# Inverse roots of the layer norms computed by Newton steps on the vector engine

## The reference, cut to what matters

```python
xn = _layernorm(x, axis=-1)
x = x + _L0_gnn_ref(xn, edge_index, ...) + _L0_mix_ref(xn[None], ...)[0]
# in _L0_gnn_ref: three times gat_conv (gather by src, softmax by dst, sum by dst), elu, layer_norm
# in _L0_mix_ref:
q = (x @ Wq + bq).reshape(...)            # k and v the same way from xn
kv = jnp.einsum('blhd,blhe->bhde', _phi(k), v)
out = attention of _phi(q) with kv, @ Wo + bo
x = _layernorm(x + out, ln1_g, ln1_b)
ff = jax.nn.relu(x @ W1 + b1) @ W2 + b2
x = _layernorm(x + ff, ln2_g, ln2_b)
```

## Time and profile before

| | |
|---|---|
| time, median of 3 runs | 7684.07 us (7683.78 to 7686.03) |
| the profiled execution: time, span | 7691.76 us, 7690.0 us |
| busy share PE, PEld, DVE, ACT, POOL | 70%, 52%, 65%, 56%, 51% |
| layer 0 message stage | about 450 to 1650 us of the span |
| layer 1 message stage | about 1950 to 3150 us |
| layer 2 message stage | about 3400 to 4600 us |

### The profile page before, as it was taken

The page is one execution under the profiler, slowest core; times in us unless marked ns, Lnnn a source line. Parts: engine busy times, 40 slices in busy tenths (PEclk is TensorE's granted clock), DMA queues, the critical chain, the costliest instruction groups (busy, mean ns, idle before and its releaser), DMA issues. The chain is left out here.

```text
span 7690.0 us, 106452 instructions
## 1 busy us (share of the span) xinstructions
PE 5415.3 (70%) x24694; PEld 4030.1 (52%) x24694; DVE 5030.4 (65%) x13781; ACT 4268.1 (56%) x13681; POOL 3924.3 (51%) x3916
## 2 busy tenths in 40 slices
PE   1757777744677777437777750899997888887678
PEld 1634444423455555325555530899994466665335
DVE  5555555666567676756666657777773387778673
ACT  4457777864688888548778773455554422111132
POOL 3276666646767677467666753000000277777322
PEclk7867788876789898768888885999998898887789
DMA  6243333333444444343433333100005644333302
GB/s 169 76 126 103 103 101 104 103 82 122 137 112 113 112 113 111 87 145 108 111 106 108 110 79 109 48 19 20 20 20 184 221 121 123 108 106 99 94 21 74
DMA packets 492760, 774.99 MB, mean 101 GB/s; under 512 B 86759, under 2 KB 368311, under 8 KB 492279
## 3 DMA queue, kind: packets, MB, share of 16 engines
q0 software_dynamic: 168240, 452.12, 21.5%
q1 hardware_dynamic: 324183, 319.65, 13.2%
HBM read 634.42 MB, written 146.27 MB: 102 GB/s over the span
## 5 line engine op out<-in xcount | busy, mean ns | idle before, releaser
L1679 POOL DMA_INDIRECT gm_got<-scratch_feat,keep_src_tab x2520 | 2503.7, 994 | 1091.7 <-issue 633.0
L1885 ACT ACTIVATE gm_got<-gm_got 128x64 f32<-128x64 f32 x10080 | 2453.1, 335 | 4.7 <-DVE gm_got L1813 4.7
L1933 PE MATMUL gm_bank<-gm_got,gm_onehot 128*128 128x264 f32 x5040 | 1844.7, 479 | 773.7 <-DVE gm_onehot L1836 429.2
L1933 PEld LDWEIGHTS gm_bank<-gm_got,gm_onehot 128*128 128x128 f32 x5040 | 1028.4, 228 | 1250.8 <-issue 647.9
L1830 DVE TENSOR_TENSOR gat_acc<-gat_acc,gm_bank 128x264 f32 x2520 | 1074.6, 426 | 706.3 <-PE gm_bank L1933 436.9
L1014 POOL DMA_INDIRECT mix1a_got<-scratch_rel_feat,layer_rel_tab x240 | 244.7, 1020 | 1397.7 <-issue 1396.7
L1014 POOL DMA_INDIRECT mix1b_got<-scratch_rel_feat,layer_rel_tab x600 | 608.6, 1014 | 190.8 <-issue 187.5
L1064 PE MATMUL mix1b_m_bank<-mix1b_got,mix1b_onehot 128*128 128x256 f32 x1200 | 398.0, 468 | 159.3 <-DVE layer_acc L1041 122.0
L1836 DVE TENSOR_TENSOR gm_onehot<-keep_iota_row,keep_dst_tab 128x896 f32<-128x896 f32 x360 | 385.7, 1080 | 27.7 <-PE gm_bank L1933 24.9
L1064 PEld LDWEIGHTS mix1b_m_bank<-mix1b_got,mix1b_onehot 128*128 128x128 f32 x1200 | 252.0, 228 | 269.6 <-DVE mix1b_onehot L1021 171.3
L3017 ACT ACTIVATE moe_h<-moe_first,moe_shift,moe_gain 128x256 f32<-128x256 f32 x400 | 203.7, 559 | 253.7 <-PE moe_first L3058 253.7
(11 more groups left out here) (559 smaller groups left out, 12232.8 us busy)
## 6 DMA issues: line engine op xcount, KB each, us to landing
scratch_rel_feat<-rel_out SPq DMA_DIRECT2D x50, 1024.0 KB, 5.5
gm_got<-scratch_feat,keep_src_tab POOLq DMA_INDIRECT x2520, 2.8
gm_flags<-scratch_flags SPq DMA_DIRECT2D x90, 280.0 KB
gf_feat<-scratch_feat SPq DMA_DIRECT2D x75, 256.0 KB, 4.1
gf_old<-scratch_hidden SPq DMA_DIRECT2D x75, 256.0 KB, 4.7
scratch_hidden<-gf_h SPq DMA_DIRECT2D x75, 256.0 KB, 3.6
scratch_feat<-gf_row SPq DMA_DIRECT2D x50, 260.0 KB, 3.5
gm_x<-scratch_x SPq DMA_DIRECT2D x50, 256.0 KB
```

Of the source, the lines that this page charges most:

```text
L1679: nc.gpsimd.indirect_dma_start(out=got[:, place // GROUPS, place % GROUPS * GROUP + j, 0:GAT_ROW], out_offset=None, in_=dram["feat"][layer ...
L1885: last = nc.scalar.activation(rows, rows, ACT.Copy, scale=got[:, b, i, D + h:D + h + 1])
L1933: nc.tensor.matmul(bank[i % BANKS][:, 0:GAT_SUM], onehot[:, i % HOTS, :], got[:, v[1] % B, i, :], start=True, stop=True).then_inc(s_sum, 1)
```

## The change

The square roots on ACT and the reciprocals on DVE go. DVE works out the inverse root itself: a first guess from the bits of the number (5 instructions: add epsilon, times -0.5, shift, conversion, subtraction), then three Newton steps of 3 instructions. Each of the 14 is counted with `Count.done`, so each waits for the one before it. They work on 128x2 values in `MixSums` and on 128x4 in `MixPairs`, where the two norms of an iteration share them.

`MixSums` puts them at slots 3, 5, 6 and 7 of each window, and copies mean and inverse root of its pair into a tile `moments` (two instructions at slot 9). `MixPairs` reads these for the first norm, so its `stats0`, `aggr0`, `root0` and first reciprocal go; the 14 instructions for the other two norms stand at slots 38, 39, 41 and 42. A tile of zeros is replaced by a part of the one-hot tile, and `mv` is set to one at the start of a stage.

```diff
+class InverseRoot:
+    PER = 14
+    PARTS = ("guess", "step1", "step2", "step3")
...
+    def part(self, nc, name, variance):
+        c, v, half, root, t, bits = self.count, self.v, self.half, self.root, self.t, self.bits
+        if name == "guess":
+            c.done(nc.vector.tensor_scalar(v[:, :], variance, LN_EPS, None, ALU.add))
+            c.done(nc.vector.tensor_scalar(half[:, :], v[:, :], -0.5, None, ALU.mult))
+            c.done(nc.vector.tensor_single_scalar(bits[:, :], v[:, :].bitcast(I32), 1, ALU.arith_shift_right))
+            c.done(nc.vector.tensor_copy(t[:, :], bits[:, :]))
+            c.done(nc.vector.tensor_scalar(root[:, :].bitcast(I32), t[:, :], -1.0, float(0x5F3759DF), ALU.mult, ALU.add))
+        else:
+            c.done(nc.vector.tensor_tensor(t[:, :], root[:, :], root[:, :], ALU.mult))
+            c.done(nc.vector.tensor_tensor(t[:, :], t[:, :], half[:, :], ALU.mult))
+            c.done(nc.vector.scalar_tensor_tensor(root[:, :], t[:, :], 1.5, root[:, :], ALU.add, ALU.mult))
...
 class MixSums:
-    DVE_AT = {0: "stats", 4: "add", 2: "aggr", 9: "scale", 19: "neg", 24: "phi"}
-    ACT_AT = {6: "root", 13: "turn", 19: "va0", 21: "exp", 23: "va1"}
+    DVE_AT = {0: "stats", 2: "aggr", 3: "guess", 4: "add", 5: "step1", 6: "step2", 7: "step3", 9: "scale", 19: "neg", 24: "phi"}
+    ACT_AT = {13: "turn", 19: "va0", 21: "exp", 23: "va1"}
...
         elif name == "scale":
-            dve.wait_ge(self.s_std, n)
-            nc.vector.reciprocal(self.rstd[:, :], self.std[:, :]).then_inc(self.s_rstd, 1)
-            dve.wait_ge(self.s_rstd, n)
...
             last.then_inc(self.s_xn, 1)
+            pair = bass.ds(it[0] * (2 * PAIR) + self.pair_no(it, t // WINDOW) * PAIR, PAIR)
+            nc.vector.tensor_copy(self.moments[:, 0, pair], self.mv[:, :, 0])
+            nc.vector.tensor_copy(self.moments[:, 1, pair], rstd[:, :])
...
-        if name == "root":
-            act.wait_ge(self.s_mv, n)
-            nc.scalar.activation(self.std[:, :], self.mv[:, :, 1], ACT.Sqrt, bias=keep["eps"][:, 0:1]).then_inc(self.s_std, 1)
...
 class MixPairs:
-    DVE_AT = {0: ["stats0"], 2: ["aggr0"], 11: ["scale0"], ...
-              ... 37: ["aggr1"], 38: ["centre1"], 40: ["centre2"],
+    DVE_AT = {9: ["scale0"], ...
+              ... 37: ["aggr1"], 38: ["centre1", "guess"], 39: ["step1"], 40: ["centre2"], 41: ["step2"], 42: ["step3"],
...
-    ACT_AT = {8: ["root0"], 15: ["turn"], 20: ["exp"], 30: ["att_turn"], 41: ["root1", "root2"], 48: ["y1_turn"],
+    ACT_AT = {15: ["turn"], 20: ["exp"], 30: ["att_turn"], 48: ["y1_turn"],
...
+            if name == "scale0":
                 dve.wait_ge(self.s_x, it[0] * 16 + (it[1] + 1) * 16)
+                for i in range(PAIR):
+                    mean, rstd = (self.moments[:, j, bass.ds(...)] for j in range(2))
+                    last = nc.vector.tensor_scalar(self.xn[:, i, :], self.x[:, i, :], mean, rstd, ALU.subtract, ALU.mult)
...
     def finish(self, dve, j, n, out, shift):
         dve.wait_ge(self.s_cen[j], n)
-        dve.wait_ge(self.s_rstd[j], n)
```

More of the change, by code:

```diff
@@ L1242, with __init__ @@
     PE_AT |= {t: [f"down{k}"] for k, t in enumerate((2, 3, 4, 5, 6, 7, 8, 9, 12, 13, 16, 17, 18, 19, 23, 24))}
-    BACK = {"add2", "stats2", "aggr2", "centre2", "finish2", "total", "root2", "relu3"} | {f"down{k}" for k in range(16)}
-    def __init__(self, nc, space, io, dram, keep, cfg, kv_sum, ones, first_pair, n_pairs):
+    BACK = {"add2", "stats2", "aggr2", "centre2", "finish2", "total", "relu3"} | {f"down{k}" for k in range(16)}
+    def __init__(self, nc, space, io, dram, keep, cfg, kv_sum, moments, ones, first_pair, n_pairs):
         sb, sem = space.sb, space.sem
@@ L1263, in __init__ @@
         self.z = sb("z", [P, PAIR * 8])
[L1264 to L1267 removed]
+        self.inverse = InverseRoot(space, 2 * PAIR)
+        self.stats = sb("stats", [P, 2, PAIR, 6])
+        self.mv = sb("mv", [P, 2, PAIR, 2])
         self.bank = [space.ps(f"side{i}", [P, 512]) for i in range(3)]
@@ L1297, in names @@
             return []
-        return [n for n in at.get(t, ()) if tags == "both" or (tags == "back") == (n in self.BACK)]
+        return [n for n in at.get(t, ()) if tags == "both" or n in InverseRoot.PARTS or (tags == "back") == (n in self.BACK)]
     def number(self, it, name):
@@ L1343, in start_dve @@
         dve.wait_ge(self.s_w, 16 * len(self.loads))
+        nc.vector.memset(self.mv[:, :, :, :], 1.0).then_inc(self.s_ones, 1)
+        dve.wait_ge(self.s_ones, 1)
         for a in range(HALVES):
@@ L1352, in dve @@
             n = self.number(it, name)
-            if name == "stats0":
+            if name == "scale0":
                 dve.wait_ge(self.s_x, it[0] * 16 + (it[1] + 1) * 16)
-                self.statistics(0, self.x)
-            elif name == "aggr0":
-                self.aggregate(dve, 0, n)
-            elif name == "scale0":
-                self.invert(dve, 0, n)
-                dve.wait_ge(self.s_rstd[0], n)
                 for i in range(PAIR):
-                    last = nc.vector.tensor_scalar(self.xn[:, i, :], self.x[:, i, :], self.mv[0][:, i, 0:1], self.rstd[0][:, i:i + 1],
-                                                   ALU.subtract, ALU.mult)
+                    mean, rstd = (self.moments[:, j, bass.ds(it[0] * PAIR + ((self.first_pair + it[1]) * PAIR + i), 1)] for j in range(2))
+                    last = nc.vector.tensor_scalar(self.xn[:, i, :], self.x[:, i, :], mean, rstd, ALU.subtract, ALU.mult)
                 last.then_inc(self.s_xn, 1)
+            elif name == "guess":
+                if tags != "back":
+                    dve.wait_ge(self.s_mv[0], it[0] + (it[1] + 1))
+                if tags != "front":
+                    dve.wait_ge(self.s_mv[1], it[0] + it[1])
+                self.inverse.enter(it[0] + (it[1] + 1))
+                self.inverse.part(nc, name, self.mv[:, :, :, 1].rearrange("p j i -> p (j i)"))
+            elif name in InverseRoot.PARTS:
+                self.inverse.part(nc, name, None)
             elif name == "neg":
@@ L1444, in finish @@
         dve.wait_ge(self.s_cen[j], n)
-        dve.wait_ge(self.s_rstd[j], n)
         for i in range(PAIR):
-            last = self.nc.vector.scalar_tensor_tensor(out[:, i, :], out[:, i, :], self.rstd[j][:, i:i + 1], shift[:, :], ALU.mult, ALU.add)
+            last = self.nc.vector.scalar_tensor_tensor(out[:, i, :], out[:, i, :], self.inverse.root[:, j * PAIR + i:j * PAIR + i + 1], shift[:, :], ALU.mult, ALU.add)
         return last
@@ L1459, in act @@
             n = self.number(it, name)
-            if name.startswith("root"):
-                j = int(name[4:])
-                act.wait_ge(self.s_mv[j], n)
-                nc.scalar.activation(self.std[j][:, :], self.mv[j][:, :, 1], ACT.Sqrt, bias=self.keep["eps"][:, 0:1]).then_inc(self.s_std[j], 1)
-            elif name == "turn":
+            if name == "turn":
                 act.wait_ge(self.s_xt, n)
@@ L1727, in _ @@
                 nc.vector.memset(ones[:, :], 1.0)
-                nc.vector.memset(zeros[:, :], 0.0).then_inc(s_zero, 1)
+                nc.vector.memset(zeros, 0.0).then_inc(s_zero, 1)
                 dve.wait_ge(s_zero, 1)
@@ L3622, in build @@
             scores, kv_sum = space.sb("scores", [P, N_TILES, 2 * GAT_HEADS]), space.sb("kv_sum", [P, HALVES, P + 1])
+            moments = space.sb("moments", [P, 2, N_TILES])
             cfg = mix_cfg(io, dram, 0)
```

77 lines of the change are left out of this document (41 added, 36 removed).

## The result

The changed kernel took 7857.63 us (median of 4, 7841.76 to 7859.63), the kernel before beside it 7683.97 us: ratio 1.0218, 95% interval 1.0205 to 1.023, or +174 us. The profiled execution took 7859.63 us with a span of 7857.8. The forecast was 7769 us (+85), in a range of 7700 to 7810: the sign was right, and the time lies outside the range.

What follows compares the result with a forecast made beforehand. No engine was full: DVE and PE, then ACT, paced layer 0, DVE's gapless stretch layers 1 and 2, with instruction-fetch stalls in layers 0 and 2. -5 + 49 + 41 = +85 us gave 7769 us, range 7700 to 7810.

Steps and rivals of the forecast that it cites:

- the sum for layers 1 and 2: Layers 1 and 2: DVE's added instructions less removed work, +1.8 us an iteration (+49 us), plus layer 1's new fetch, +41 us.
- The 14 instructions: DVE, dependent instructions at 0.19 us each: 2.65 us for 14, all lengthening the gapless stretch in layers 1 and 2.
- The new fetch in layer 1: DVE's longer loop body must begin to fetch in layer 1: 3.4 us at each of 12 back branches, +41 us.
- three stay and four don't: A DVE loop touching three instruction packets of about 127 records stays in instruction memory; one touching four is fetched anew.
- the late second packet: Upper bound on the fetch price per back branch: 4.0 us, if layer 2's second packet is late too.
- Layer 0: Layer 0's windows: +1.1 us from DVE's steps, -1.28 from the load, -0.2 a window times 25: -5 us.
- the credit of 1.28 us a window for the load at slot 20: Layer 0: ACT's table load at slot 20 is on the path, so removing it gives -1.28 us a window.
- ACT: 155 table loads (199 us) go; worth nothing in layers 1 and 2, where ACT waits longer for DVE.
- Layers 0 and 2: Their DVE loops fetch already at each back branch and go on doing so.
- Rivals B to E: B no fetch 7728 0.17; C layer 2 holds 7697 0.08; D layers 0+2 hold 7663 0.06; E ACT paces 7456 0.05.
- The marks I named: Profile after: layer 1 has 12 DVE gaps of about 2.7 us, five to six packets an iteration; ACT's wait at least 9.4.

Runs made afterwards that it cites:

- layer 0's part alone: Kernel before with Newton steps and kept moments in `MixSums` only, `MixPairs` as before, 20 unused increments ahead of layer 1's loop: 7690.57 us, ratio 1.0004.
- the kernel placed at (0, 3, 63): Changed kernel with 3 unused semaphore increments on DVE ahead of layer 1's loop and 63 ahead of layer 2's: 7815.26 us, ratio 1.0172.
- places 12 to 17: Changed kernel with 6 and 64, 8 and 64, or 5 and 68 unused increments ahead of layers 1 and 2: ratios 1.0099, 1.0091 and 1.0105.
- the kernel before with its three loops placed: Kernel before with 45, 80 and 105 unused semaphore increments ahead of the loops of layers 0, 1 and 2: 8637.09 us, ratio 0.9938; 0.9924 when repeated.
- 371 records: Changed kernel, semaphore of the 14 instructions cleared once an iteration in layers 1 and 2, both loops placed by pads 6 and 73: ratio 1.0132.

## Why the prediction was wrong, step by step

**The failed step is the sum for layers 1 and 2.** "Together +1.8 us an iteration, 27 iterations: +49 us" and "Price: layer 2's iteration against layer 1's, 3.4 us" added small costs to an iteration as if its length could take any value, and both costs were too low. With the same stop, layer 2 rose by 3.35 us where 1.8 was charged (+43 us in its stage against 22). Layer 1 rose by 10.1 us where 5.2 was charged (+128 against 68). Those two differences, 21 and 60 us, are 81 of the 83 by which the spans miss the forecast (+168 against +85).

**The 14 instructions** were mis-sized at the timeline: 3.9 us for 2.65, by 0.15 us at L1088 and by the waits behind the four groups. With 3.9 in its place the forecast's own sum (less 0.52 for the two reciprocals and 0.3 in the first window) gives +3.1 us, near the 3.35 measured in layer 2. So the size alone is a rival to the steps as an account of layer 2. Against it: taking 0.74 us of those waits away gave nothing, and taking away three instructions, some 0.8 us by that account, gave nothing in layer 2 and 0.6 in layer 1. None of the 14 gives 81.8 us in layer 2, the length before, and not 0.5 to 0.8 under it, where a sum would put it. That they are on the path in both layers was right.

**The new fetch in layer 1** came as forecast, because the body (383 records; I had 385 to 390) no longer holds. In part this was luck: by "three stay and four don't" 383, just under 384, would have held at one or two places, and it held at none that was tried, since the fetch runs on past the branch. The price was too low: I took layer 2's, with one packet behind the branch, and left the late second packet as a bound (4.0 us). It was 6.7 us an iteration instead of 3.4 (10.1 less layer 2's 3.35): a stop that grew by 3.8 us, to 4.15, and PE at the lower clock for the start of the second window, for which the other 2.9 us are left. That term, PE's clock, the forecast put at nothing. Placed elsewhere, the surplus is gone (85.3).

**Layer 0,** forecast -5 us: -4.6 in the kernel after, -12 with layer 0's part alone. That the size came out is luck: the same layer 0 gives two results 8 us apart, and the credit of 1.28 us a window for the load at slot 20 is not borne out, since the loads were worth nothing in the run without them. **ACT** was right: its loads left the loops, its wait at slot 48 grew from 6.04 to 14.55 us in layer 2 (at least 9.4 forecast), and the time did not fall. **Layers 0 and 2** went on fetching, as forecast. Rivals B to E fell: layer 1's iteration is not near 80, layer 2's not below 81, layers 0 and 2 still fetch, and the loads are worth nothing.

**The marks I named** came out in part: there are 12 stops in layer 1, five to six packets an iteration in layers 1 and 2 (six to seven in layer 0) and ACT's longer wait. The stops have 4.15 us and not 2.7, and "about 83.7 us, like layer 2's" was off in both layers, which is the mark that carried the time.

What stays open: what makes the steps. That PE's clock makes the third is shown by the iterations of the kernel after that differ in it (86.1 and 88.7 to 89.4 us), by the kernel placed at (0, 3, 63), whose stretch has 0.94 or 0.95 in each of the four iterations looked at, and by the last trip of layer 1 with layer 0's part alone. Why the clock stayed low in these and not in the others isn't. That the first two steps come from it too is argued only, and length and mean clock aren't tied one to one: 81.9 us came with 0.88 in layer 2 of the kernel before and with 0.90 in layer 2 with layer 0's part alone.

On the slower chips the means show no such steps, since trips of one loop differ by up to 8 us, but the trips do: of the 63 trips of layers 1 and 2 at places 12 to 17, 52 lie within 0.6 us of 95.6, 98.9 or 102.1 us, again 3.2 to 3.3 us apart. There a loop changes its length from trip to trip, and its mean can lie anywhere between.

A version that beats both kernels is the kernel before with its three loops placed: 0.9938 and 0.9924 on two chips. I can't credit all of it to the stops. Some 20 us of it lie in the first mixing stage of the later part (three iterations of 84 to 88 us, where the unplaced kernels on the slower chips have 87 to 96), and the two unplaced kernels beside the first placed one fetch the same 16 or 17 packets there as it does; that part wasn't settled.

## What to carry to other kernels

Count the records of an engine's loop and where it begins before adding small instructions to it: 20 increments that do nothing cost some 47 us here and 230 saved some 51. In a loop whose trips are all of one length, do not add a fraction of a microsecond to it and multiply: look whether the lengths seen in sister loops lie on steps, and ask to which one the surplus carries. Look at PE's granted clock trip by trip, too: it alone made trips of the same code 3 us longer. Removing work from an engine that waits for another (199 us of table loads) is worth nothing, and paying for it on the engine that it waits for is worth less than nothing.

## What the runs showed of the hardware

DVE's instructions were fetched in packets of 8 KB, some 128 records (0.31 MB over 38 packets, which come 125 to 128 records apart in layer 2 of the kernel before). Bodies of 363 and 371 records stayed where they fitted in three packets; a body of 383 stayed at none of the places tried. At places 14 to 17 a packet was asked for 7 records ahead of the branch. The Trainium skill ("TensorE: Matmul & The Clock Gate", Architectural detail: the array is 16× 32×32, not 1× 128×128) gives VectorE a queue of 8. That fits the number; that it is the cause no run shows.

A stop took 2.8 to 3.2 us where one packet came right behind the branch (places 14 to 17 and the middle of a packet). Where two came it fell with the place: 4.15 us at 7, 3.8 at 9, 3.56 at 10, 3.34 at 12. PE's clock stayed at 1.2 GHz through 9.2 us without idle time in nine of twelve iterations of one loop (0.50), and in the same loop placed three records further it was back early (0.94 or 0.95).

A multiplication with -0.5 of a 128x4 tile took 0.31 us where its neighbours took 0.16, and 0.17 on a 128x2 tile in layer 0; why, no run asked.
